# Earlier joins between the stages of an attention-and-transformer kernel, and row copies cut into 112 and 15 partitions

## The reference, cut to what matters

```python
# x is (16, 512, 128)
xn = layernorm(x)
x = x + attn(xn) + ffn(xn)
# attn: 16 heads of 64, causal
logits = (q @ k.T + causal + pos_bias) / 64
attn = softmax(logits) @ v @ Wo + bo
# ffn: two layers (DEPTH = 2), x here being xn; 8 heads of 64, windows of 64
def shift_token(t):                 # second half of the columns comes from the row before
    t1, t2 = split(t, 2); return concat([t1, pad(t2, one row down)[:-1]])
h = shift_token(x); q, k, v = split(h @ wqkv, 3)
q, k = rotary_xpos(l2norm(q) * qs, l2norm(k) * ksc)
x = x + local_attention(q, k, v) @ wo        # a window sees itself and the window before
h = layernorm(shift_token(x)) * lg + lb
a, g = split(h @ w1 + b1, 2)
x = x + (a * gelu(g)) @ w2 + b2
```

## Time and profile before

| | before |
|---|---|
| median of 3 runs | 2703.7 us (2702.74 to 2705.8) |
| the profiled execution's own time | 2707.02 us |
| its span, first to last instruction | 2705.2 us |
| mean granted clock of TensorE | 0.977 |
| busy, PE / DVE / ACT / POOL | 2547.8 / 2009.4 / 2158.3 / 1629.7 us |
| transfers, mean | 28 GB/s; 80196 of 128513 packets under 512 B |

### The profile page before, as it was taken

One profiled execution on the slowest core, in us unless ns is written; L12 is line 12 of the kernel. 1 busy time (PEld: TensorE's weight loads), 2 busy tenths in 40 slices (PEclk: granted clock), 3 DMA queues, 4 the chain that ended last, 5 costly groups with the idle time before them and its releaser, 6 DMA issues. The chain is left out here.

```text
span 2705.2 us, 71234 instructions
## 1 busy us (share of the span) xinstructions
PE 2547.8 (94%) x24208; PEld 1988.1 (73%) x24208; DVE 2009.4 (74%) x5647; ACT 2158.3 (80%) x6335; POOL 1629.7 (60%) x1947
## 2 busy tenths in 40 slices
PE   7999999999999999999599999997979999999796
PEld 4777777777777777777378888885767888888575
DVE  4666666666666666666389999995659999999565
ACT  5888888888888888888389999996438999999642
POOL 3444444444444444444389999994229999999521
PEclk8999999999999999999799999998989999999898
DMA  2000000000000000000311111111111111111112
GB/s 72 7 7 10 9 9 5 8 7 9 9 9 5 10 7 7 9 6 5 103 41 41 38 42 39 38 42 46 33 26 40 38 42 42 38 40 42 46 33 79
DMA packets 128513, 77.07 MB, mean 28 GB/s; under 512 B 80196, under 2 KB 110736, under 8 KB 128144
## 3 DMA queue, kind: packets, MB, share of 16 engines
q1 hardware_dynamic: 127968, 72.34, 10.9%
q10 hardware_dynamic: 176, 0.07, 0.0%
HBM read 17.58 MB, written 8.41 MB: 10 GB/s over the span
## 5 line engine op out<-in xcount | busy, mean ns | idle before, releaser
L306 POOL TENSOR_SCALAR L<-L,rinv 128x128 f32<-128x128 f32 (+3 forms) x1024 | 522.4, 533 | 622.7 <-DVE rinv L488 622.7
L370 ACT ACTIVATE L<-L,nmax 128x384 f32<-128x384 f32 (+3 forms) x1024 | 571.8, 561 | 144.2 <-DVE nmax L474 144.2
L474 DVE CUSTOM_DVE_ANT_0 L<-bank,bias_tab 128x256 f32<-128x256 f32 (+3 forms) x1024 | 470.5, 479 | 180.3 <-PE bank L590 178.3
L886 ACT ACTIVATE f_L<-bank,f_nmax,f_rn 128x128 f32<-128x128 f32 x1024 | 459.9, 486 | 5.0 <-DVE f_nmax L1013 5.0
L863 POOL TENSOR_TENSOR f_rn<-f_ssq,f_mhalf 128x16 f32<-128x16 f32 x128 | 419.1, 3274 | 18.2 <-DVE f_ssq L997 4.7
L845 POOL TENSOR_TENSOR f_qkr<-f_ab 128x256 f32<-128x256 f32 x512 | 414.3, 838 | 10.3 <-DVE f_ab L964 10.3
L611 PE MATMUL bank<-ident,L 128*128 128x128 f32 x2560 | 370.4, 276 | 2.3 <-DVE PT L215 2.0
L611 PEld LDWEIGHTS bank<-ident,L 128*128 128x128 f32 x2560 | 296.8, 141 | 83.4 <-issue 46.1
L964 DVE TENSOR_TENSOR f_ab<-bank,f_tab 128x512 f32<-128x512 f32 x512 | 347.8, 680 | 8.8 <-ACT f_sq L876 8.8
L632 PE MATMUL bank<-PT,v 128*64 128x512 f32 (+3 forms) x2048 | 303.9, 439 | 0.6 <-DVE yacc L507 0.4
L632 PEld LDWEIGHTS bank<-PT,v 128*64 128x64 f32 x2048 | 126.8, 136 | 166.2 <-issue 164.9
(11 more groups left out here) (145 smaller groups left out, 6390.8 us busy)
## 6 DMA issues: line engine op xcount, KB each, us to landing
f_vm<-f_v SPq DMA_DIRECT2D x224, 128.0 KB, 2.4
f_hs<-xf SPq DMA_DIRECT2D x132, 32.0 KB
f_hs<-xf SPq DMA_DIRECT2D x132, 31.8 KB
xb<-in_L_attn_x SPq DMA_DIRECT2D x16, 256.0 KB, 2.8
out<-yacc SPq DMA_DIRECT2D x32, 128.0 KB, 1.8
f_hs<-xf SPq DMA_DIRECT2D x32, 128.0 KB
out<-f_acc SPq DMA_DIRECT2D x4, 1024.0 KB, 7.5
f_hs<-xf SPq DMA_DIRECT2D x32, 127.0 KB
```

What stands on the lines that cost most here:

```text
L306: nc.gpsimd.tensor_scalar(t, t, rinv[:, h % RING, a, i:i + 1], 1.0, ALU.mult, ALU.mult).then_inc(s_N, 1)
L370: nc.scalar.activation(t, t, ACT.Exp, bias=nmax[:, ep % RING, a, i:i + 1], scale=-1.0, accum_out=rsum[:, ep % RING, a, i:i + 1]).then_inc( ...
L474: nc.vector.tensor_tensor_reduce(out=L[:, p % RING, a, LOFF[i]:LOFF[i] + (i + 1) * P], in0=ps_s[a][i], in1=bias_tab[:, 2 * p + a, T - (i + ...
L886: nc.scalar.activation(L[:, ot % 2, a, k, :], ps_s[a][:, k * P:k * P + P], ACT.Exp, bias=nmax[:, ot % 2, a, k:k + 1], scale=rn[:, ot % 2, ...
```

## The change

- Stage 1: in slot p = 4 ACT writes `v` and `xT_hi` earlier, and DVE writes `xT_lo` ahead of the addition to `yacc`. POOL builds the masks in slot (0, 6); SP loads the shifted rows of batch 0 in batch 1, and the first layer's weights and table in batch 15 (into rows of the bias table that are no longer read, `w["rows"]`); POOL rounds the weights and makes the table in the last slots (`prepare_attention`). The block that prepared is gone.
- The loop over layers is written out twice (`for l in range(DEPTH)`).
- `local_attention` loads MLP rows of batches 0 and 1 at b = 4 and 5, reads `out` back at b = 6 of layer 0, and in its draining slots does the first steps of the MLP for batch 0 (statistics, normalising, transposes, scaling, rounding), the statistics of batch 1 and the rounding of w1.
- `gated_mlp` has four buffers of rows; PE's order is `hidden(0)`, `hidden(1)`, transposes, all of `second`, `hidden(2)`; in layer 0 it loads and prepares layer 1's attention; in layer 1 POOL adds `xf` into `acc` batch by batch, DVE adds the last product there, and ACT's queue stores each batch of 256 KB one slot later. The last block is gone.
- Each copy of 127 partitions is two transfers, of 112 and of 15 partitions.

```diff
+SHIFTED = ((1, 113), (113, P))
@@ causal_attention, SP
+                if b == B - 1:
+                    sp.wait_ge(s_L, at(b, 8 * HP, 8 * 4))
+                    for part in range(3):
+                        load_attention_weights(sp, c, d, w, 0, part, w["s_load"])
+                if b == 1:
+                    ...
+                    for t in range(TT):
+                        load_shifted(sp, c["hs"], xf, 0, t, w["attn"][f"hs{t}"])
@@ causal_attention, POOL
+                if (b, p) == (0, 6):
+                    build_masks(nc, pool, c, w)
+                for n in {(B - 1, 6): (0, 1, 2), (B - 1, 7): (3, 4, 5), (B, 0): (6, 7)}.get((b, p), ()):
+                    ...
+                    prepare_attention(nc, pool, c, w, n, w["s_load"])
@@ load_shifted and load_shifted_batch
-    sp.dma_start(hs[1:P, t, half:D], x_t[0:P - 1, half:D]).then_inc(s_hs, 16)
+    for lo, hi in SHIFTED:
+        sp.dma_start(hs[lo:hi, t, half:D], x_t[lo - 1:hi - 1, half:D]).then_inc(s_hs, 16)
...
-    sp.dma_start(hs[1:P, r, :, half:D], x_b[0:P - 1, :, half:D]).then_inc(s_hs, 16)
+    for lo, hi in SHIFTED:
+        sp.dma_start(hs[lo:hi, :, half:D], x_b[lo - 1:hi - 1, :, half:D]).then_inc(s_hs, 16)
@@ local_attention, SP, POOL, ACT, DVE, PE
+            if b in (4, 5) and t == 0:
+                ...
+                load_shifted_batch(sp, w, xf, b - 4)
+            if (l, b, t) == (0, 6, 0):
+                sp.dma_start(w["acc"][:], d["out"].rearrange("b (t p) d -> p (b t) d", p=P)).then_inc(w["s_acc"], 16)
+            if (b, t) == (B, 1):
+                batch_scale(nc, pool, w, 0)
+            if (b, t) == (B, 2):
+                pool.wait_ge(sem["weights"], 16 * 12)
+                nc.gpsimd.tensor_copy(w["w1_hi"][:], c["w1"][:]).then_inc(w["mlp"]["w_hi"], 1)
+                ...
+            if (b, t) == (B + 1, 0):
+                batch_low(nc, pool, w, 0)
+                batch_affine(nc, act, c, w, 0)
-        nc.vector.tensor_copy(w_hi[:], c["wqkv"][:]).then_inc(sem["w_hi"], 1)
+            if (b, t) == (B, 0):
+                batch_statistics(nc, dve, w, 0)
+            if (b, t) == (B, 2):
+                batch_normalise(nc, dve, w, 0)
+                batch_statistics(nc, dve, w, 1)
+            if (b, t) == (B, 3):
+                batch_transposes(nc, pe, c, w, 0)
@@ gated_mlp
+            if 2 <= b < B:
+                sp.wait_ge(sem["hn"], at(b, TT, -3 * TT))
+                load_shifted_batch(sp, w, xf, b)
+            if l < DEPTH - 1 and 7 <= b < 15:
+                prepare_attention(nc, pool, c, w, b - 7, sem["weights"])
+            if l == DEPTH - 1 and now is not None:
+                ...
+                nc.gpsimd.tensor_tensor(a, a, xf[:, b * TT:b * TT + TT, :], ALU.add).then_inc(sem["acc"], 1)
+            if l == DEPTH - 1 and four is not None:
+                act.wait_ge(sem["x_out"], four + 1)
+                act.dma_start(d["out"].rearrange("b (t p) d -> p (b t) d", p=P)[:, four * TT:four * TT + TT, :],
+                              w["acc"][:, four * TT:four * TT + TT, :]).then_inc(w["s_stored"], 16)
...
-        with nc.Fori(0, DEPTH) as l:
+        for l in range(DEPTH):
```

More of the change, by code:

```diff
@@ L251, in _ @@
                 sp.wait_ge(s_out[half], 16 * B)
+            sp.wait_ge(w["s_load"], 16 * 5)
+            for t in range(TT):
+                sp.wait_ge(w["attn"][f"hs{t}"], shifted_count(t))
         @block.gpsimd
@@ new lines, in batch_scale, with batch_transposes @@
+def batch_scale(nc, pool, w, b):
+    pool.wait_ge(w["mlp"]["ve"], b + 1)
+    nc.gpsimd.tensor_tensor(w["rstd"][:], w["ve"][:], w["mhalf"][:, 0:TT], ALU.pow).then_inc(w["mlp"]["rstd"], 1)
+def batch_transposes(nc, pe, c, w, b):
+    sem, ps_t = w["mlp"], c["bank"][6]
+    pe.wait_ge(sem["hn"], TT * (b + 1))
+    pe.wait_ge(sem["hT_hi"], b)
+    for t in range(TT):
+        last = nc.tensor.transpose(ps_t[:, t * P:t * P + P], w["hn"][:, t, :], c["ident"][:])
+    last.then_inc(sem["T_done"], 1)
@@ L1183, in _ @@
-        for t in range(TT):
-            sp.wait_ge(w["attn"][f"hs{t}"], shifted_count(t))
-        sp.wait_ge(sem["weights"], 64)
+            if 2 <= b < B:
+                sp.wait_ge(sem["hn"], at(b, TT, -3 * TT))
+                load_shifted_batch(sp, w, xf, b)
+            if nxt is not None and 4 <= b < 7:
+                load_attention_weights(sp, c, d, w, nxt, b - 4, sem["weights"])
+            if nxt is not None and 7 <= b < 11:
+                sp.wait_ge(sem["x_out"], 1)
+                load_shifted(sp, c["hs"], xf, 0, b - 7, w["attn"][f"hs{b - 7}"])
@@ L1207, in _ @@
+            if now is not None and b > 0:
+                batch_scale(nc, pool, w, b)
+            if l < DEPTH - 1 and 7 <= b < 15:
+                prepare_attention(nc, pool, c, w, b - 7, sem["weights"])
+            if l == DEPTH - 1 and now is not None:
+                pool.wait_ge(w["s_acc"], 16)
+                a = w["acc"][:, b * TT:b * TT + TT, :]
+                nc.gpsimd.tensor_tensor(a, a, xf[:, b * TT:b * TT + TT, :], ALU.add).then_inc(sem["acc"], 1)
         batch_slots(pool, slot, 3)
@@ L1295, in hidden, with second @@
                     nc.tensor.matmul(ps[0:n, :], w1_hi[:, col], hT_lo[:, r, :], start=False, stop=True).then_inc(sem["ga_done"], 1)
-            def second(tiles):
-                for t in tiles:
+            def second():
+                for t in range(TT):
                     for j in range(3):
@@ L1310, in slot @@
             hidden(0)
+            if two is not None:
+                pe.wait_ge(sem["H"], at(two, 3, -1))
+            hidden(1)
+            if one is not None and one > 0:
+                batch_transposes(nc, pe, c, w, one)
             if three is not None:
@@ L1313, in slot @@
                 pe.wait_ge(sem["x_out"], at(three, 1, 0))
-                second(range(2))
-            if one is not None:
-                pe.wait_ge(sem["hn"], at(one, TT, TT))
-                pe.wait_ge(sem["hT_hi"], at(one, 1, 0))
-                for t in range(TT):
-                    last = nc.tensor.transpose(ps_t[:, t * P:t * P + P], hn[:, t, :], ident[:])
-                last.then_inc(sem["T_done"], 1)
-            if three is not None:
-                second(range(2, TT)).then_inc(sem["y_done"], 1)
+                second()
             if two is not None:
                 pe.wait_ge(sem["H"], at(two, 3, 0))
-            hidden(1)
             hidden(2)
```

380 lines of the change are left out of this document (198 added, 182 removed).

## The result

The changed kernel takes 2639.94 us (median of 4 runs, 2634.75 to 2640.46), against 2704.75 us for the kernel before on the same chip: ratio 0.9756, 95% interval 0.9739 to 0.9773. The profiled execution took 2640.46 us, 66.6 us less than the profiled one of before, where I had forecast 80.5; its span is 2638.6 us. So the time is in the range and 17 us above the forecast of 2623.

| from, to | before | after | gain | my sum |
|---|---|---|---|---|
| start, last addition to `yacc` | 1315.13 | 1308.15 | 7.0 | 8.3 |
| first projection of layer 0 | 26.83 | 5.14 | 21.7 | 21.9 |
| 60th addition to `xf` | 497.97 | 511.88 | -13.9 | -1.0 |
| 64th and last addition (the draining slots) | 25.45 | 31.62 | -6.2 | -2.8 |
| first hidden column | 12.97 | 1.63 | 11.3 | 11.0 |

What follows compares the result with a forecast made beforehand. Bound by four kinds of join between stages, where PE does next to nothing, plus repeated waits in stage 1 and the MLP. Terms sum to 80.5 us off the profiled 2707.0; by medians 2623 us, range 2604 to 2642.

Steps and rivals of the forecast that it cites:

- Stage 1 into layer 0: From stage 1's last addition to layer 0's first projection: preparation moves into earlier slots, projection at 1320.1 not 1341.96, gaining 21.9 us.
- Slot p = 4: Stage 1, 15 times: DVE writes `xT_lo` before adding `yacc`, so PE waits 0.55 us less each time, gaining 8.3 us.
- Attention into MLP: Twice: batch 0's chain moves into draining slots; last addition 2.8 us later, PE's hidden columns earlier, gaining 8.2 us a layer.
- The MLP: Middle slots fall from 8.04 to 7.5 us with rows loaded earlier: gains 6.0 and 7.5 us, cold clock -2.4.
- Layer 0 into layer 1: From layer 0's last addition to layer 1's first projection: 10.05 us shrink to 2.4, gaining 7.6 us (bounds 5 and 8).
- The end: After the last addition: 19.5 us shrink to a last store and block end of 3.3, gaining 16.2 us.
- The read-back: Reading `out` (4 MB) in batch 6 holds SP's queue some 15 us, but rows are asked for ahead: costs 1 us.
- Hidden costs: Attention's tiles: one more transfer per tile costs its issue on SP, which is mostly waiting; no us subtracted for it.
- The joins give back more: Rival, 0.19: operations put into draining slots hold whole chains and PE drops to half clock; 14 us less gain, 2637 us.
- The split doesn't help: Rival, 0.08: copies of 112 + 15 take as long as 127, MLP batches stay at 8.04 us; 18 us in all, 2641 us.
- Slower: Rival, 0.03: the layers' written-out code supplies instructions too slowly and stretches every tile; decides above 0.65 us a tile.

## Why the prediction was right, and where it was not

- **Stage 1 into layer 0**, 21.9: 21.7. The chain of transpose, rounded part and subtraction took 1.2 us, for which I had put 1.3.
- **Slot p = 4**, 8.3: from one `xT_lo` to the next 79.02 us and not 79.64, 0.62 over 14 distances, 8.7; the 0.55 was right. The stretch shows only 7.0, since this execution's first `xT_lo` came 1.8 us later (12.35 against 10.55), which varies from run to run (10.73 in the experiment with one copy, whose stage 1 is otherwise the same).
- **Attention into MLP**, 16.4: 8.1 (5.2 and 2.9). This is the first step that failed. Its second half was right, hidden columns 1.6 and 2.1 us after the last addition, 11.3 and 10.9 us gained for 11.0. The first half, "the last addition comes 2.8 later", was 6.2 and 8.0. "Normalising (taken like the four statistics, 1.1)" is what that operation takes beside an idle GpSimd; at this place I had myself put GpSimd's rounding, and it took 3.72. The last tile's second reciprocal starts 5.25 us after the first, and with both operations behind it 1.76: they cost 3.5 there, for which I had put 1.2. The other part is the clock after PE's wait, for which I had put nothing. In layer 0 the last two steps take 10.61 and 5.33 us against 5.85 and 3.59, which is 3.0 more than those 3.5. In layer 1 PE was at half clock once more, ahead of it (granted 0.60 from 2492 to 2496, that step 9.42 us and not 7.82); why there, stays open. With both operations moved behind the chain the delay is -0.3 and 2.2, so the 1.6 that I had put for the statistics of batch 0 isn't seen in layer 0.
- **The MLP**, 13.5 less 2.4 for the clock: 17.9. A slot is 7.28 and not 7.5, which over 14 slots and two layers is 6.2 of the 6.8. I had subtracted from 8.04 only the 0.48 that the row shows ahead of `second`. But a PE row's idle time counts from the modelled end of the matmul ahead, 0.40 us after its start, while the next one can start 0.23 after it; with the first matmul's longer fill the wait cost 0.76. Start to start, `second` came 0.88 us after the last hidden matmul, and 0.24 in the kernel before with the split alone; its first matmul took 0.38 and not 0.27. The mechanism, rows, was right, though I gave PE's order and the buffers a part in it that they don't have. PE ran at half clock in layer 0's first 2.6 us (granted 0.50) and not in layer 1's (1.00). One sum is off by 0.1: the parts of an MLP add up to 122.05 and not 122.2.
- **Layer 0 into layer 1**, 7.6: 8.5. **The end**, 16.2: 16.8, the span ending 2.7 us after the last addition.
- **The read-back**, 1, bounds 0 to 3: 12.9. This is the second step that failed, and the larger. "They are asked for 2 to 3 tiles ahead" is wrong: the copy that was held was issued at 1498.72, and PE stood from 1507.13 (1517.05 less 9.92), so it is asked for 8.4 us ahead, one tile. The rest of that tile's rows were issued only from 1512.84 on, when the queue was free. The wait of 9.9 became 12.9 since PE came back at half clock, a cost that the term left out as well. I had taken the lead from the order of the code; in the trace of before, the copy of a tile is issued some 9.5 us ahead of the transpose that reads it.
- **Hidden costs**: the tiles take 7.85 us and not 7.83, 1.2 us a layer. They do with one copy too, and in the kernel before with the split alone they take 7.83, so the additional transfer isn't the cause; which it is stays open.
- **The rivals.** "The joins give back more" gave 14 us for other reasons than the read-back, of which 8 came; its own parts (8.4, 3 and 5.3, if slot p = 4 is to give 3) add up to 16.7. "The split doesn't help" was priced at 18 us; the experiment with one copy says 61. The 128 that it sets against its 137 stands nowhere in the sum, whose MLPs are about 126 and 125: by the prediction's own terms the price was some 23, and it left out attention. The rival was false, but had it been true, my 2641 would have been wrong by 60. "Slower" needed 0.65 us a tile; 0.02 came.

Together: -11.9 for the read-back, -8.3 for the joins into the MLP, +6.8 in the MLP, and -0.6 for all others are the 14 us by which the profiled gain is below the sum. The other 3 of the 17 us come from going over to medians: I took 3.3 off for the profiled execution of before, and that of the changed kernel lies only 0.5 above its median. That the time still fell into the range is in part luck: the MLPs' surplus of 6.8 us stood against 20 us of misses, and without it the time would have been about 2647.

## What to carry to other kernels

Count the partitions of a copy behind which the queue is stuck and look at their divisors: 112 and 15 (or 126 and 1) are fast where 127 and 113 are not, and a queue that is stuck behind such a copy holds everything that is put behind it later. A large transfer costs what it holds up in its own queue: cut it, or give it a queue in which nobody waits (small transfers beside it still land several us late), and read off the trace how far ahead of its use the next small transfer is issued. Work moved into a draining pipeline belongs behind the last tile's chain on its engine, and its duration is that beside its new neighbours, not that of its old place. Put the half clock after a long wait of PE into the price of the wait: here it added a third to it.

## What the runs showed of the hardware that I had not expected

- Behind a copy of 113 partitions the next issue on SP's queue takes 5.7 to 5.9 us, behind one of 127 it takes 6.9, and copies of 126 and 1 are both issued in 1.6 (layer 1's MLP, four rows a partition). Behind a copy of 127 partitions with one row each it takes 0.86.
- While the queue is stuck, 0.08 of the 16 engines is busy; with 112 partitions it is 0.92.
- With the 16 engines busy nine tenths and more for 14 us by one transfer, rows from another queue landed up to 8.3 us after their issue (1.9 is usual) and held PE for 0.30 us; from the same queue they took 16.3 and held it for 9.92.
- VectorE's `f_ve` of 4 elements a partition took 1.25 us and not 0.17 beside a GpSimd subtraction, and ended with it; four normalisings took 1.11, 1.83 or 3.72 us by what GpSimd did.
- After a wait of 9.92 us PE's granted clock was 0.54 over the next 7 us.
